# Identity products on TensorE ahead of three stretches of an attention and mixture-of-experts kernel

## The reference

```python
x = x + xattn(layernorm(x), ctx, Wq, Wk, Wv)          # 32 heads of 16; q and k RMS-normed; softmax over 512 keys
x = x + moe(layernorm(x), ...)                        # below

gate = xt @ Wr + br                                   # 7 routed experts
ids  = top_k(gate + gate_bias, 2)
probs = softmax(gate at ids)
u = xt @ Wup + bup;  g = silu(u @ Wgate + bgate) * u;  eo = g @ Wdown + bdown     # each 512 x 512
out = sum over the two experts of probs * eo  +  the same three products of one shared expert for every token
```

## Time and profile before

| | |
|---|---|
| median of 3 runs | 1018.86 us (1018.45 to 1020.17) |
| profiled execution, its own time | 1018.88 us |
| its span, from the first to the last instruction | 1017.1 us |
| mean granted TensorE clock | 0.986 |
| PE, matmuls | busy 960.4 us (94%), 6730 instructions |
| PEld, weight loads | 698.0 us (69%) |
| DVE | 703.6 us (69%) |
| ACT | 498.4 us (49%) |
| POOL | 230.6 us (23%) |

### The profile page before, as it was taken

The page is one execution under the profiler, slowest core; times in us unless marked ns, Lnnn a source line. Parts: engine busy times, 40 slices in busy tenths (PEclk is TensorE's granted clock), DMA queues, the critical chain, the costliest instruction groups (busy, mean ns, idle before and its releaser), DMA issues.

```text
span 1017.1 us, 18058 instructions
## 1 busy us (share of the span) xinstructions
PE 960.4 (94%) x6730; PEld 698.0 (69%) x6731; DVE 703.6 (69%) x1442; ACT 498.4 (49%) x614; POOL 230.6 (23%) x223
## 2 busy tenths in 40 slices
PE   3999999999999999985999999999999999999995
PEld 3634443454444554332999999899998998999995
DVE  5788767876688657764579775765857677757653
ACT  3577668855786658875233222422424243424211
POOL 1122012420132201321000000232333332333321
PEclk9999999999999999998799999999999999999998
DMA  9100100010000100301341214363363535544523
GB/s 342 73 1 2 42 1 1 22 64 1 1 2 21 63 1 1 105 21 42 99 153 55 72 46 183 74 190 59 74 186 73 175 64 168 167 108 111 144 56 41
DMA packets 28985, 78.94 MB, mean 78 GB/s; under 512 B 7040, under 2 KB 7040, under 8 KB 24832
## 3 DMA queue, kind: packets, MB, share of 16 engines
q1 hardware_dynamic: 18400, 52.31, 14.4%
q0 software_dynamic: 10528, 25.87, 12.8%
HBM read 57.64 MB, written 20.52 MB: 77 GB/s over the span
## 4 chain that ended last, share of the span: by engine, by line
PE 49%; DVE 2%; issue 1%; DVEq 0%; POOL 0%; ACT 0%; POOLq 0%
PE u_ps L1188 16%; PE z_ps L1188 15%; PE y_ps L1188 15%; PE xt_ps L1201 2%; PE z_ps L1182 1%; DVE w_sb L1390 1%; PE y_ps L1214 0%; DVE stats L1406 0%; DVE u_lo L1551 0%; DVE x_lo L1400 0%; DVEq L1032 0%; DVE y_sb L1579 0%; POOL out L1132 0%; PE xt_ps L1174 0%; ACT u_hi L1322 0%
## 5 line engine op out<-in xcount | busy, mean ns | idle before, releaser
L646 ACT ACTIVATE probs<-scores 128x2048 f32<-128x2048 f32 x128 | 240.6, 1879 | 75.8 <-PE scores L322 72.8
L1188 PE MATMUL u_ps<-x_hi,w_sb 128*128 128x256 f32 x896 | 167.9, 285 | 5.2 <-issue 3.0
L1188 PE MATMUL z_ps<-u_hi,w_sb 128*128 128x256 f32 x896 | 169.1, 287 | 0.2 <-DVE u_lo L1551 0.2
L1188 PEld LDWEIGHTS u_ps<-x_hi,w_sb 128*128 128x128 f32 x896 | 143.1, 194 | 8.0 <-issue 4.6
L1322 ACT ACTIVATE u_hi<-u_ps,b_ug 128x256 fp32r<-128x256 f32 x112 | 47.0, 471 | 204.0 <-PE u_ps L1188 204.0
L1188 PEld LDWEIGHTS z_ps<-u_hi,w_sb 128*128 128x128 f32 x896 | 142.4, 193 | 0.4 <-DVE u_lo L1551 0.4
L1188 PE MATMUL y_ps<-w_sb,g_hi 128*128 128x512 f32 x448 | 138.8, 391 | 0.4 <-DVE g_lo L1569 0.4
L338 PE MATMUL o_ps<-probs,v_sb 128*17 128x512 f32 x1024 | 134.8, 598 | 1.0 <-ACT probs L646 1.0
L1188 PE MATMUL u_ps<-x_lo,w_sb 128*128 128x256 f32 x448 | 127.7, 285 | 0.0
L1188 PE MATMUL z_ps<-u_lo,w_sb 128*128 128x256 f32 x448 | 127.2, 284 | 0.0
L1551 DVE SCALAR_TENSOR_TENSOR u_lo<-u_ps,b_ug,u_hi 128x256 fp32r<-128x256 f32 x112 | 49.0, 479 | 80.7 <-ACT u_hi L1322 80.0
(11 more groups left out here) (218 smaller groups left out, 1585.5 us busy)
## 6 DMA issues: line engine op xcount, KB each, us to landing
w_raw<-w_all SPq DMA_DIRECT2D x27, 1024.0 KB, 7.0
ctx_raw<-ctx_t SPq DMA_DIRECT2D x4, 1024.0 KB, 6.8
out<-x_sb SPq DMA_DIRECT2D x16, 256.0 KB, 2.0
xg<-xn_dram POOLq DMA_DIRECT2D x14, 256.0 KB, 3.1
x_sb<-x SPq DMA_DIRECT2D x1, 3072.0 KB, 18.1
xn_dram<-xn SPq DMA_DIRECT2D x12, 256.0 KB, 2.1
bd<-b_down SPq DMA_DIRECT2D x9, 256.0 KB, 4.2
x_sb<-x SPq DMA_DIRECT2D x4, 256.0 KB, 3.7
```

Source lines behind the costliest of these rows:

```text
L646: nc.scalar.activation(probs[:, t % 2], scores[:], ACT.Exp).then_inc(p_ready, 1)
L1188: ins = nc.tensor.matmul(out_ps, stat[a], mov[b], start=(first and a + b == 0), stop=(last and a == 1), skip_group_check=True)
```

## The change

Four runs of products are put into PE's list whose results nobody reads. Each multiplies `ident` by `ident`, 128 columns, plain float32, into a PSUM place that holds nothing at that time: 52 at the opening into `tr`, behind the wait for `ident_set`; in the second block, into `y_ps`, 20 before `x_transposes(0)`, 7 behind it, and 7 inside `last_gates` behind the second `norm_transposes` and ahead of the first `gates`. None of them waits for a semaphore of its own, and none raises one. No other engine's list changes.

```diff
@@ first block, PE
             pe.wait_ge(ident_set, 1)
+
+            for _ in range(52):
+                nc.tensor.matmul(tr[:, 0:P], ident[:], ident[:], start=True, stop=True, skip_group_check=True)
             pe.wait_ge(blocks_set, 3)
             k_turns(0, 0, 6)
@@ second block, PE
+            def idle_products(count):
+                for _ in range(count):
+                    nc.tensor.matmul(y_v[:, 0, 0:P], ident[:], ident[:], start=True, stop=True, skip_group_check=True)
+
             def last_gates():
                 for t in range(BT):
                     norm_transposes(t)
+                    if t == 1:
+                        idle_products(7)
                     if t:
                         gates(t - 1)
                 gates(BT - 1)
 
+            idle_products(20)
             x_transposes(0)
+            idle_products(7)
             tile(0, 0, behind_up=last_gates)
```

## The result

The changed kernel takes 1015.14 us (median of 10 runs, 1012.58 to 1017.13), the kernel before 1018.41 us (10 runs, 1017.16 to 1020.17): ratio 0.9966, 95% interval 0.9954 to 0.9977, so 0.34% faster: 3.5 us by the ratio, 3.3 between the two medians. The forecast was 1013.7 us in 1011.3 to 1016.8. The profiled execution took 1015.44 us, span 1013.7, mean granted clock 0.991 (0.986 before).

What follows compares the result with a forecast made beforehand. PE was taken to bound the second block and the attention, slowed by its lower clock in places. Gains of 1.2 + 1.95 + 1.95 + 0.1 = 5.2 us took 1018.9 to 1013.7 us, range 1011.3 to 1016.8.

Steps and rivals of the forecast that it cites:

- The opening: Ahead of K: 52 products raise the clock for K and the transposes; net gain 0.9 to 1.8 us, 1.2 taken.
- the price: Time per identity-product instruction at full clock: between 0.109 and 0.12 us, the upper taken.
- the overrun: Opening: products end 0.1 to 1.0 us after K could have begun at 14.92, paid in full.
- Of the attention I take the same.: Attention: PE bounds it, with few gaps and no DMA waited for after the opening.
- The head: Second block's start: up projection 5.76 instead of 7.82 us, less 0.1: gain 1.95 us.
- The gates: Last gates to z: seven products fit exactly and cost nothing; the stretch gains 1.95 us with a fall, up to 3.6 without.
- The case taken: Gates: transposes don't count, so the clock falls at 494.5 to 495 and z starts slow; 1013.7 us, chance 0.48.
- The sum: Whole kernel: opening 1.2, head 1.95, gates 1.95 and z 0.1 give 5.2 us, from 1018.9 to 1013.7.
- the second rival: Opening overruns by 2 us or more, gates fall early and stay low into z: some 2.5 us, 1016.4; chance 0.15.

Runs made afterwards that it cites:

- the second block alone: Changed kernel without the opening's 52 products, the other 34 kept: 1014.76 us, ratio 0.9956 to the kernel before.
- the head alone: Only the 20 and 7 products around tile 0's transposes added to the kernel before: 1016.23 us, ratio 0.9972.
- wide products alone: Kernel before with all router products 112 columns wide instead of 7, no identity product: 1015.68 us, ratio 0.9966.
- the opening alone: Only the opening's 52 products added to the kernel before: 1019.33 us, ratio 1.0005.
- the two with wide products: Whole change with all router products wide: 1014.23 us, ratio 0.9950; opening's 52 products with wide products in the attention only: 1016.99 us, 0.9981.
- wide products with 52 and with 46: Whole change plus router products 112 columns wide, with 52 opening products: 1014.23 us, ratio 0.9950; with 46: 1012.26 us, 0.9933.
- 72 products: Changed kernel with 72 instead of 52 products at the opening: 1021.03 us, ratio 1.0019 to the kernel before.

## Why the prediction was right, and where not

**The opening.** Right in mechanism; the size agrees by luck. The clock rises some 4 us after the first product, as reckoned; with the change of pace near 5.7 us, some 19 go slowly and 85 in 9.5 us, 0.112 us each: nearer to the lower bound of the price (0.109) than to the 0.12 that I took. So in this pair of traces the overrun is 0.3 instead of 1.0 us and the gain 1.76 where 1.2 was taken (range 0.9 to 1.8). The pair flatters it: in the trace of before the context arrived later than in any other without products at the opening. Four traces have the opening of before (that one, the second block alone, the head alone, wide products alone), and four have the 52 products (the change, the opening alone, the two with wide products). K begins at 13.67 to 14.92 us in the first four and at 15.01 to 16.01 in the others, on average 1.3 us later; from K to the first exponential it is 26.2 to 27.0 us and 24.8. The first exponential comes at 40.84 us on average (40.02 to 41.76) and at 40.32 (39.78 to 40.76). That is 0.5 us and not 1.76: the products give 1.8 us by the clock and cost 1.3 by their overrun, since the context is ready before 14.92 us in four of the six traces that show it, and since the 104 instructions take 13.4 to 14.4 us, as the clock rises sooner or later. The prediction took one trace's 14.92 as the time at which K could begin.

**"Of the attention I take the same."** This step failed. I took the attention as a stage that passes the opening's gain on, because its clock was 1.00 and PE had few gaps. The runs showed that it holds six pairs of gates behind which the clock can fall without PE being idle, 0.8 to 1.5 us each time. With the opening's products they are met more often: no run of the opening alone has the mean clock that most runs of before have. That every one of the twelve has its fall behind gates is inferred from these clocks; five profiles show falls in place, one of them without the opening's products. The opening alone gave 0.0 us. With the attention's gates wide it gave 1.9, but the trace has only 0.57 of them at the attention's end. Nor was there as much to pass on as one pair of traces said, by the averages above.

**The head.** Right: transposes at 479.22 and `xl_done` as forecast (u at 482.16, 7.48 us behind the entry; reckoned 7.6), u in 5.86 instead of 7.82 us. That the clock could fall before the products had hold was named with 1.5 us; it did so in four of the later traces (the head alone, wide products with 52 and with 46, 72 products), at 1.1 to 1.3 us each.

**The gates.** The case taken, a fall in the stretch behind the seven products, is the one that came: at 493.9 where 494.5 to 495 was written (its own distances of 3.4 to 3.7 us give 494.3 to 494.7), z from 497.60, 4.1 us earlier than before if the entry's own 0.26 is left out (3.9 reckoned), and z in 7.20 us (6.6 reckoned). The reason was half wrong. I counted transposes and 7-column products alike, with the rule of the Trainium skill behind it; the transposes do count, and the 0.50 of 498 to 500 us, read as agreement, stood over 7-column products alone (from 497.13 to 500.40 in that trace). And the seven products, which I gave credit for carrying the clock, weren't needed in the trace of the head alone. That the stretch took 7 us instead of 9 goes with where the clock fell: 3.1 to 3.7 us behind the first gates in every trace with the head's products and 7 columns, and 0.9 to 1.0 us behind them before and with the opening alone. But the run with wide products in the attention only, without any product in the second block, had 3.7 us and a stretch of 6.89 us too. So these 2 us can't be put down to the products for certain; what decides where the fall comes stays open.

**The sum.** 5.2 us were forecast and 3.3 to 3.5 measured. The second block gave 3.67 of the 4.0 reckoned for it. Most of the rest is the opening's 1.2, of which 0.3 arrived. The time lies midway between the forecast and the second rival (less arrives than reckoned), with its loss in this trace in another place than that rival named: not in the overrun and not at the gates of tile 0, but inside the attention.

## What to carry to other kernels

A clock of 1.00 in one trace is no guarantee for a stage: look for runs of matmuls with few moving columns, which keep PE occupied and yet let the clock fall, and widen their moving operand with copies as far as this takes hardly longer (here 16 instructions took 2.04 us with 112 columns and 1.95 with 7); this costs no instruction and here was worth as much as 86 filler products. Filler products pay where PE would stand still anyway, and every one that is still running when real work is ready is paid in full, so leave them short of the earliest arrival, taken from several traces and not from one. A gain at the front of a program has to be followed to its end: it shifts everything behind it, and what it meets there can cost as much.

## What the runs showed of the hardware

- 16 instructions of 7 columns (1.95 us, PE occupied throughout) were followed by a clock of 0.50 for 3.4 us at six places in five of seven profiles of the attention; with 112 columns (2.04 us) they never were, in five profiles.
- Float32 transposes of 128x128 raised the clock from 1.2 to 2.4 GHz and held it as float32 products did (6 to 7 and then 11 or 12 to the microsecond at the opening; 40 of them in 4.56 us at the head), here with an identity, nearly all zeros, as both operands.
- The time at which the first context is ready moves from 13.7 to 15.2 us among the traces in which K waits for it; single profiles of two openings can't be compared more closely than that.
- Runs of one program fall into groups by how many falls they meet: with the change 1012.6 us at a mean clock of 0.994, 1014.9 to 1015.4 at 0.991, 1016.9 to 1017.1 at 0.988 to 0.990.
